# Four message-passing layers on one core: fewer one-hot picks, and messages multiplied ahead of the scan

## What is computed

```python
h = relu(layernorm(x)); x = x + L0(h)   # msg = relu([h[dst], h[src], ea32] @ W1 + b1) @ W2 + b2 ; sum over dst
h = relu(layernorm(x)); x = x + L1(h)   # softmax over dst of edge_weight1; sum of weight * h[src]; elu
h = relu(layernorm(x)); x = x + L2(h)   # (h[dst]-h[src]) @ theta.T + theta_b + phi(h)[src]; max over dst
h = relu(layernorm(x)); x = x + L3(h)   # relu(relu([h[src], h[dst], ea16] @ W1 + b1) @ W2 + b2) @ W3 + b3 ; mean over dst
```

## Time and profile before

| | |
|---|---|
| median of 3 runs | 9926.22 us (9922.42 to 9931.58) |
| profiled execution | 9931.22 us, span of its trace 9930.0 us |
| busy, share of the span | PE 65%, PEld 43%, DVE 45%, ACT 20%, POOL 64% |
| mean granted TensorE clock | 0.745 of full speed |
| POOL's gathers | 3136 in layers 0 and 3, 2842 in layers 1 and 2, 946 ns each |
| HBM | 70 GB/s over the span |

### The profile page before, as it was taken

How to read it: one execution, slowest core, us unless ns; L and a number is a source line. 1 busy time by engine, 2 the same in 40 slices (tenths; PEclk the granted TensorE clock), 3 DMA queues, 4 the chain that set the end, 5 groups by cost and what they waited for, 6 DMA issues and landing times.

```text
span 9930.0 us, 72794 instructions
## 1 busy us (share of the span) xinstructions
PE 6424.3 (65%) x20160; PEld 4312.5 (43%) x20160; DVE 4508.3 (45%) x6769; ACT 1960.4 (20%) x4698; POOL 6342.4 (64%) x6675
## 2 busy tenths in 40 slices
PE   0466766766366766676556666766605888888883
PEld 0355555555234444443334444443403555555552
DVE  5244444444544444444554444444543444444443
ACT  4122222222111111111210000000002333333331
POOL 6666666666666666666556666666576666666665
PEclk9766666666577878887667777877856888888876
DMA  7344333334222222222212222222213333333332
GB/s 258 69 84 87 85 86 85 87 84 87 57 52 58 57 60 57 60 57 59 49 42 52 52 50 50 54 50 52 51 33 66 80 79 82 79 80 80 81 79 49
DMA packets 1039760, 699.44 MB, mean 70 GB/s; under 512 B 600467, under 2 KB 946981, under 8 KB 1039237
## 3 DMA queue, kind: packets, MB, share of 16 engines
q1 hardware_dynamic: 808400, 475.49, 17.5%
q0 software_dynamic: 214864, 177.10, 12.4%
q10 hardware_dynamic: 16100, 42.20, 1.1%
HBM read 456.38 MB, written 237.76 MB: 70 GB/s over the span
## 4 chain that ended last, share of the span: by engine, by line
issue 29%; PE 17%; another core or an unknown queue 14%; DVE 7%; POOL 3%; ACT 3%; DVEq 0%; DMA 0%; ACTq 0%; POOLq 0%; SPq 0%
PE pRows L854 4%; POOL R L596 2%; PE pOdd L842 2%; PE pEven L842 2%; DVE S L1122 2%; PE pT L823 2%; PE pOdd L800 2%; PE pOdd L835 2%; PE pEven L835 2%; PE pRows L800 2%; ACT H L703 1%; DVE pT L1103 1%; DVE H L1083 1%; POOL first_rows L545 1%
## 5 line engine op out<-in xcount | busy, mean ns | idle before, releaser
L582 POOL DMA_INDIRECT G<-table,idx x3136 | 2966.4, 946 | 1565.4 <-issue 866.5
L582 POOL DMA_INDIRECT G<-table,e_dst x2842 | 2688.0, 946 | 1593.2 <-issue 869.3
L1033 DVE TENSOR_TENSOR_SCAN K<-mask_f,K,pT 48x512 f32<-48x512 bf16 x784 | 1008.0, 1286 | 2623.0 <-remote 1438.4
L854 PEld LDWEIGHTS pRows<-w,S 128*128 128x128 f32 x6272 | 1603.4, 328 | 567.2 <-issue 523.7
L854 PE MATMUL pRows<-w,S 128*128 128x48 f32 x6272 | 1459.5, 388 | 0.4 <-DVE S L1045 0.4
L800 PE MATMUL pRows<-h,K 128*128 128x343 f32 x2072 | 748.0, 516 | 525.4 <-issue 393.7
L823 PE MATMUL pT<-ident,G 128*112 128x128 f32 x3136 | 654.7, 348 | 646.7 <-DMA G<-first_rows 349.2
L800 PE MATMUL pRows<-e_all,K 128*128 128x336 f32 x2072 | 744.7, 509 | 350.0 <-issue 259.0
L823 PEld LDWEIGHTS pT<-ident,G 128*112 128x112 f32 x3136 | 548.8, 195 | 949.4 <-issue 650.9
L800 PE MATMUL pOdd<-e_all,K 128*128 128x336 f32 x2044 | 732.0, 509 | 328.5 <-issue 231.4
L800 PE MATMUL pOdd<-h,K 128*128 128x343 f32 x2044 | 716.1, 503 | 305.4 <-issue 192.3
(11 more groups left out here) (166 smaller groups left out, 6168.7 us busy)
## 6 DMA issues: line engine op xcount, KB each, us to landing
mask_f<-same_row SPq DMA_DIRECT2D x392, 256.0 KB
prefix<-O SPq DMA_DIRECT2D x392, 256.0 KB
G<-first_rows SPq DMA_DIRECT2D x784, 96.0 KB
prefix<-O SPq DMA_DIRECT2D x392, 192.0 KB
G<-table,idx POOLq DMA_INDIRECT x3136
G<-table,e_dst POOLq DMA_INDIRECT x2842
first_rows<-zeros ACTq DMA_DIRECT2D x14, 2688.0 KB
K<-in_ea_dram SPq DMA_DIRECT2D x588, 64.0 KB
```

The source lines that it names most:

```text
L582: pool.indirect_dma_start(rows[:, slot, j, 0:widths[l]], None, table[l], bass.IndirectOffsetOnAxis(ap=at[:, n, j:j + 1], axis=0))\
L854: last = pe.matmul(o, s[:, :, j], (w2_0 if l == 0 else w3_3)[:, :], start=True, stop=True)
L1033: dve.tensor_tensor_scan(K[r, c.slot, :], mask_of(c, r), pT[c.slot % 2][r, :], K[r, (c.slot - 1) % RING, CHUNK - 1:CHUNK], ALU.mult, ALU.add)\
```

## The change

In layers 1 and 2 one column of 32 (slot 3) is picked in place of three, so POOL gathers 31 columns a turn in place of 29. Groups are of ten blocks (`PICK_SPAN`), ten groups of them, one product of up to 490 or 480 columns per group. Four PSUM banks take the sums in turn (`PICK_SUMS`), and the one-hot ring has three entries. The group's number is worked out in the setup with a few more DVE operations. The masks of a half turn come by one DMA, not four. DVE's stages there are in the order pick, mark, turn out, turn in, scan.

In layers 0 and 3 the last weights are multiplied before the scan. `relu_1` or `relu_2` writes to `H1` in SBUF, the new `make_messages` multiplies W2 or W3 (128 x 48) by the chunk's 512 hidden columns, DVE scans the 48 partitions of messages, and `make_rows` only transposes the scanned 48 x 512 in four pieces. `copy_src` now waits for `dst_spread`, not for `transposed`. On PE the order is layer 1 of k-1, transposes of k, (layer 2 of k-1), rows of k-3, messages of k-2; on DVE scan of k-3, spread of k; on ACT rows out of k-4, relus of k-1, source copy of k. SP's loads of a pair all wait for `scanned` and count on one semaphore. Many waits that others imply are left out.

```diff
-PICK_GROUPS = 7
-PICK_SLOTS = (1, 4, 6)
+PICK_SPAN = 10
+PICK_SLOTS = (3,)
-PICK_RING = 4
+PICK_RING = 3
+PICK_SUMS = 4
...
                 def copy_src(c, l=l):
-                    act.wait_ge(transposed[l], c.n + 1)
-                    if not (c.fixed and c.n < RING):
-                        act.wait_ge(hidden1[l], c.n - (RING - 1))
+                    act.wait_ge(dst_spread[l], c.n + 1)
...
                     for g in range(PICK_GROUPS):
-                        for k in range(2):
-                            first = g * SPAN + k * HALF_SPAN
-                            last = pe.matmul(pick_sum[i % 2][:, k, 0:HALF_SPAN * widths[l]],
-                                             onehot[:, i % PICK_RING, g, :],
-                                             node_rows[:, first:first + HALF_SPAN, :].rearrange("p b d -> p (b d)"),
-                                             start=g == 0, stop=g == PICK_GROUPS - 1)
+                        first, stop = g * SPAN, min((g + 1) * SPAN, B)
+                        last = pe.matmul(pick_sum[i % PICK_SUMS][:, 0:(stop - first) * widths[l]],
+                                         onehot[:, i % PICK_RING, g, :],
+                                         node_rows[:, first:stop, :].rearrange("p b d -> p (b d)"),
+                                         start=g == 0, stop=g == PICK_GROUPS - 1)
...
+                def make_messages(c, l=l):
+                    pe.wait_ge((relu1 if l == 0 else relu2)[l], c.n + 1)
+                    w, hidden = (w2_0, H1[:, c.slot % 4, :]) if l == 0 else (w3_3, H1[:, 2 + c.slot % 2, :])
+                    pe.matmul(message_bank(c, l)[0:D, :], w[:, :], hidden, start=True, stop=True)\
+                      .then_inc(messages[l], 1)
...
                     for j in range(TJ):
-                        o = pO[c.slot % 2][:, j * w:(j + 1) * w]
-                        last = pe.matmul(o, s[:, :, j], (w2_0 if l == 0 else w3_3)[:, :], start=True, stop=True)
+                        last = pe.transpose(rows_bank(c, l)[:, j * D:(j + 1) * D], s[:, :, j], ident[0:D, 0:D])
...
-                stages = {0: [(0, transpose_rows), (1, layer_1), (3, make_rows)],
-                          3: [(0, transpose_rows), (1, layer_1), (3, make_rows), (1, layer_2)]}[l]
+                stages = {0: [(1, layer_1), (0, transpose_rows), (3, make_rows), (2, make_messages)],
+                          3: [(1, layer_1), (0, transpose_rows), (1, layer_2), (3, make_rows), (2, make_messages)]}[l]
...
-                stages = {0: [(0, spread_dst), (2, scan)],
-                          1: [(0, mark_nodes), (PICK_AHEAD - 1, pick), (PICK_AHEAD, turn_in),
-                              (PICK_AHEAD + 1, scan_streams), (PICK_AHEAD + 2, turn_out)],
+                stages = {0: [(3, scan), (0, spread_dst)],
+                          1: [(PICK_AHEAD - 1, pick), (0, mark_nodes), (PICK_AHEAD + 2, turn_out),
+                              (PICK_AHEAD, turn_in), (PICK_AHEAD + 1, scan_streams)],
```

More of the change, by code:

```diff
@@ L336, in build @@
         hidden2 = per_layer("hidden2_", (3,))
+        messages = per_layer("messages", MLP)
         relu2 = per_layer("relu2_", (3,))
@@ L698, in relu_1 @@
                     if l == 0:
-                        act.activation(bank[:, :], bank[:, :], ACT.Relu, bias=b1_0[:, :]).then_inc(relu1[l], 1)
+                        act.activation(H1[:, c.slot % 4, :], bank[:, :], ACT.Relu, bias=b1_0[:, :]).then_inc(relu1[l], 1)
                         return
-                    if not (c.fixed and c.n < 4):
-                        act.wait_ge(hidden2[l], c.n - 3)
-                    act.activation(H1[:, c.slot % 4, :], bank[:, :], ACT.Relu, bias=b1_3[:, :])\
+                    act.activation(H1[:, c.slot % 2, :], bank[:, :], ACT.Relu, bias=b1_3[:, :])\
                        .then_inc(relu1[l], 1)
@@ L816, in transpose_rows @@
                     if c.at_pair_start:
-                        pe.wait_ge(first_in[c.pair], ((0 if l == 0 else TURNS) + c.turn + 1) * 32)
-                    if not (c.fixed and c.n < 2):
-                        pe.wait_ge(dst_spread[l], c.n - 1)
-                        pe.wait_ge(src_copied[l], c.n - 1)
+                        earlier = 0 if l == 0 else TURNS * PAIR_LOADS[0]
+                        pe.wait_ge(pair_in[c.pair], earlier + (c.turn + 1) * PAIR_LOADS[l])
                     o = pT[c.slot % 2][:, :].rearrange("k (p j) -> k p j", j=TJ)
@@ L827, in layer_1 @@
                     pe.wait_ge(src_copied[l], c.n + 1)
-                    pe.wait_ge(dst_spread[l], c.n + 1)
-                    if c.at_pair_start:
-                        pe.wait_ge(ea_in[l][c.pair], (c.turn + 1) * (32 if l == 0 else 16))
-                    if not (c.fixed and c.n < 2):
-                        pe.wait_ge(relu1[l] if l == 3 else scanned[l], c.n - 1)
                     k = KROWS[l]
@@ L1023, in spread_dst @@
                 def spread_dst(c, l=l):
-                    if c.at_pair_start:
-                        dve.wait_ge(mask_in[c.pair], ((0 if l == 0 else TURNS) + c.turn + 1) * 16)
                     dve.wait_ge(transposed[l], c.n + 1)
-                    if not (c.fixed and c.n == 0):
+                    if c.n and c.n < 3:
                         dve.wait_ge(dst_spread[l], c.n)
-                    if not (c.fixed and c.n < RING):
-                        dve.wait_ge(hidden1[l], c.n - (RING - 1))
                     r = slice(64, 64 + D)
@@ L1037, in scan @@
                 def scan(c, l=l):
[L1039 to L1040 removed]
+                    dve.wait_ge(messages[l], c.n + 1)
+                    if c.n + 3 <= NCH:
+                        dve.wait_ge(dst_spread[l], c.n + 3)
+                    else:
                         dve.wait_ge(scanned[l], c.n)
[L1042 to L1046 removed]
+                    r = slice(0, D)
+                    dve.tensor_tensor_scan(S[r, c.slot % 4, :], mask_of(c, r), message_bank(c, l)[r, :],
+                                           S[r, (c.slot - 1) % 4, CHUNK - 1:CHUNK], ALU.mult, ALU.add)\
                        .then_inc(scanned[l], 1)
@@ L1093, in turn_in @@
                 def turn_in(c, l=l):
-                    if l == 2 and c.slot in PICK_SLOTS:
+                    if l == 2 and c.n < 3 and c.slot in PICK_SLOTS:
                         dve.wait_ge(picked[l], picks_before(c.n + 1))
@@ L1100, in turn_in @@
                         dve.wait_ge(gathered[c.slot], gathered_by(l, c))
-                    if not (c.fixed and c.n < 2):
-                        dve.wait_ge(scanned[l], 2 * (c.n - 1))
                     dve.transpose(by_half(pT[c.slot % 2][:, 0:W4]),
@@ L1109, in scan_streams @@
                     if c.slot % CH == 0:
-                        dve.wait_ge(stream_mask_in[c.slot // CH], ((l - 1) * TURNS + c.turn + 1) * (16 * QUADS))
-                    dve.wait_ge(turned_in[l], c.n + 1)
-                    if not (c.fixed and c.n == 0):
-                        dve.wait_ge(scanned[l], 2 * c.n)
-                    if not (c.fixed and c.n < 4):
-                        dve.wait_ge(turned_out[l], c.n - 3)
+                        dve.wait_ge(stream_mask_in[c.slot // CH], ((l - 1) * TURNS + c.turn + 1) * 16)
+                    if c.n == 0:
+                        dve.wait_ge(turned_in[l], 1)
                     m = mask_f if l == 1 else mask_h
```

131 lines of the change are left out of this document (58 added, 73 removed).

## The result

The changed kernel takes 10075.5 us (median of 4 executions, 10064.8 to 10080.4) against 9924.3 for the kernel before (4 executions): a ratio of 1.0151, 95% interval 1.0133 to 1.0168. The profiled execution spans 10079.2 us, 149 more than before's 9930.0.

What follows compares the result with a forecast made beforehand. POOL's gathers were taken as the floor, held above it by late results in all four layers. 9930 less 217, 229, 295 and 0 (layers 1, 2, 0, 3), plus 1 around the span, gave 9190 us; range 8870 to 9560.

Steps and rivals of the forecast that it cites:

- POOL's floor: All layers: POOL cannot go below 1.25 us a gather; 1920 us in layer 0, 1899 in layers 1 and 2.
- I take the full saving, as PE's load falls to a third: Layers 1 and 2: one pick a turn lets POOL run at its pace, saving 217 and 229 us.
- 19 + 34 = 53 us: Layers 1 and 2: lateness, some 50 us, a sum must exceed to stop POOL: pick's distance plus POOL's lead over `turn_in`.
- the picks do not release POOL: Rival, layers 1 and 2: one sum still later than the ring covers; 9636 us, chance 0.03.
- the lower bound of my term: Layers 1 and 2: nothing saved, because the sum still comes late enough to set the turn.
- the 122 us that my own working holds: Layers 1 and 2: 98 extra gathers at 1.25 us cost 122 us in each layer, counted in the saving.
- I choose POOL's 5.0: Layer 0: results come promptly, so a chunk takes POOL's 5.0 us; 1920 us, 295 saved.
- taken unchanged at 5.7 us a chunk: Layer 3: the middle between POOL's 5.0 and 6.23 with late time, nothing gained; bounds 306 us saved, 178 lost.
- its rival: All four layers at POOL's pace, layer 3 by its high-clock step of 4.08 us; 8884 us, chance 0.24.
- The rule of the Trainium skill: Layer 3: sustained PE work releases 2.4 GHz, so added products pay for themselves, giving a 4.08 us step.
- Prices of PE's pieces: Layers 0 and 3: messages' product 1.71 us low clock, 0.86 high, like layer 1's; four transposes of rows 0.85 together.
- slower: Rival, layers 0 and 3: third product at the low clock plus unshortened late results; 10792 us, chance 0.08.

Runs made afterwards that it cites:

- free batch: Batch of runs in which engines' results come promptly, programs unchanged: kernel before 8512 to 8532 us, changed kernel 8760.6 us, ratio 1.0289.
- held: Batches of runs in which engines' results come late, programs unchanged: kernel before 9919 to 9932 us or 10081, changed kernel 10075.5 us.
- experiment 1: Changed kernel; layers 0, 3: 512-column products stream 64; layer 1: no picks; layer 2: one group per sum, not ten. 9939.1 us (kernel before 9922.8).
- experiment 3: Changed kernel with one gathered column per chunk instead of four in layers 0, 2 and 3, layer 1 unchanged: 7414.1 us.
- experiment 2: Changed kernel; layer 0's first product and layer 1's sums doubled, ten products after each layer 2 sum, layer 3's messages at 64 columns: 10286.6 us.
- four picks: Kernel before with four picks a turn instead of three, 28 gathers: 8394.0 us free, ratio 0.9858; 10024.5 held, kernel before 10081.4.
- the chains: Separate kernel, twelve sections of dependent small ACT, DVE and PE operations beside gathers, memsets, transfers or nothing: 972.9 and 971.6 us free, 1215.6 held.

## Why the prediction was wrong, point by point

**POOL's floor** of 1.25 us a gather was right, and so were the stages worked out from it, to the microsecond: 1920, 1899 and 1899 us, in the free batch. The floor was never where the kernel stood in the held one.

**Layers 1 and 2: the step that failed is "I take the full saving, as PE's load falls to a third".** It made lateness a function of PE's load, though I had written that the cause could not be seen. Experiments 1 and 3 show the reverse: a tenth of PE's records left the stage at 2141 us, a quarter of the gathers made all sums prompt. The sums even came later than before: from the end of a mark to its pick it is 34.7 us in the mean of layer 1, where the kernel before had 24.0, although PE did a third of the work. I also priced the rival too low by its threshold, twice. I took 28 us, one case, for the worst seen, beside a wait of 35.9 us in the earlier trace rows. And I said that a sum must be late by more than 19 + 34 = 53 us. But POOL is already ahead of `turn_in` when a mark is made. The mark of the sum that is picked at 3712.24 above ended at 3668.5, and POOL stopped at 3705.0, 36.5 us later. In 29 of layer 1's 49 turns POOL stopped between mark and pick, in nearly all of them 32 to 38 us after the mark. The slack is the ring's gathers from where POOL already is, some 36 us, not 53. So "the picks do not release POOL", which got 0.03, is what happened; even the lower bound of my term, nothing, was missed by 31 and 25 us.

**Why it loses.** One turn of layer 1 in held batches took 44.2 us with no pick (32 gathers), 43.8 with one, 43.2 with three. So a pick more makes a turn 0.3 to 0.4 us shorter, far less than the 1.25 us of the gather that it saves, and two sums fewer saved less than two gathers more cost. In free batches the price is plain: 98 gathers x 1.25 us in each layer, the 122 us that my own working holds, times two. Measured, 246 us. The change removes what was hidden (PE's and DVE's work) and adds to what was not.

**Layer 0: "I choose POOL's 5.0"** failed in the held batch: 2208 us. I had seen that results are prompt for some 8 us after PE's pause, and concluded that PE should pause more often. But POOL pauses there too:

```profile
413.74 0.95 POOL L582 DMA_INDIRECT G<-table,idx  x1 [2.53 <-PE pT L823]
```

From then until 428.4 it gathers without a pause, and the first late results are those of the products whose records end at 424.26, 10.5 us in the earlier trace rows. In the free batch the choice is right, 1920.

**Layer 3** was taken unchanged at 5.7 us a chunk and came to 6.04, inside its bounds of 5.0 and 6.23. The columns of the messages' product explain 44 of the 100 us (experiment 2 cut them to an eighth and got 2322); the other 56 I have not tracked. In the free batch the layer takes 1960 us at a granted clock of 0.99, its rival. Without the third product, as in the kernel before, it had 0.88 there and took POOL's time as well (four picks, free batch):

```profile
6278.00:8234.30 1956.30, 1733.58 (x6224) 1223.23 (x6224) 999.60 (x780) 874.19 (x1557) 1478.68 (x1568) 0.88 0.42 92
```

So the clock did rise with the changed layer, and it bought nothing. The rule of the Trainium skill that I had set beside it (TensorE: Matmul & The Clock Gate, "The two states you'll see": sustained work releases the clock) agrees in kind; my reading of it by the share that PE's records cover does not, since 0.99 came with 84% and 0.88 with 89%. In the held batch the clock rose from 0.81 to 0.86 and the stage got longer all the same; with less work at a clock of 0.51 (experiment 1) it took 2244.

**Prices of PE's pieces.** The messages' product takes 1.06 us at the high clock, layer 1's beside it 1.13 (two records each, with their overlap), so it does measure about what layer 1's does. The four transposes of rows take 0.68, where I said 0.85.

**The rivals and chances.** The result, 10075.5, lies outside the range of 8870 to 9560. Its combination, no layer gains, had no rival of its own: I let layers 1 and 2 and layers 0 and 3 fail separately, though all four showed the same signature (POOL above its floor by a similar share, results late by an unseen cause). So the chance of a loss of this size lay nowhere, and that the time came near 10000 owes nothing to the rival "slower", whose mechanism (the third product at the low clock) was not what happened. One cause for all four would have made "nothing gained anywhere, the added work paid" a leading case.

## What to carry to other kernels

When several stages stand above a floor by the same share, suspect one cause for all of them, and don't book as saved what an unexplained wait costs now: price the change for the case that the wait stays and for the case that it was never there (here both were slower). An engine that waits for X may wait for what Z does to X, so take work away from X and from Z in turn, and look at an engine that has no part in either. And where the same program has two times, run a known kernel beside each measurement.

## What the runs showed of the hardware

- In some batches indirect gathers at 1.25 us a piece, without a pause, slow ACT, DVE and PE to one instruction per 1.40 us (ACT 0.37 to 1.40, DVE 0.25 to 1.40, a PE product 0.75 to 5.6), after 4 to 26 us. A step of 1.52 us left the chains untouched. In other batches, on two of the same chips too, nothing of it is seen. Busy times of ACT and DVE don't grow in the trace (ACT's scaling 0.33 us, DVE's spread 1.29, held and free); only starts and completions move.
- The gathers themselves are not late: by the packets of their queue they land 2.3 to 2.5 us after their issue, in the mean of each full stage of the changed kernel in a held batch as in a free one, with at most four under way. So the transfers do not queue.
- Most semaphore updates by gathers are missing from held traces: the changed kernel's has 22773 of 109776, the free one 109697. In experiment 3 the stages with one gather a chunk have 95 to 100% of them, layer 1 has 9%. In the held chains the section with a step of 1.52 us has 93%, every section with a step of 1.25 us 5 to 19%, and beside SP's plain transfers none is missing. The pages show it as a missing time to landing, held and then free:

```profile
G<-table,idx POOLq DMA_INDIRECT x3136
G<-table,idx POOLq DMA_INDIRECT x3136, 2.5
```

So the loss goes with the slowing, and a releaser that a held trace names, "issue" and "remote" above all, may hide an update that was not recorded.
- What makes a batch held stays open, and so does the mechanism. No run here could set it. One rival is untested: every execution on record has a granted clock, so a trace was taken in each, and whether taking it is what holds the engines in some batches no run tells.
- PE's records in the trace can end tens of microseconds before the result is out: a sum's 20 records ended at 3731.5, its semaphore was updated at 3757.37 and the pick started at 3757.40.
